# Last part of a graph network kernel: four neighbouring vertices to a partition, the last step on GpSimd, the load ring filled at once

## What is computed

```python
# out: the convolution, (B, N, H); top1[b]: the expert of graph b; x: the layer's input (after the first layer norm)
s = jax.ops.segment_sum(out.sum(axis=1), top1, num_segments=n_exp)
ss = jax.ops.segment_sum((out * out).sum(axis=1), top1, num_segments=n_exp)
mean = s / cnt                       # one column of channels per expert
var = ss / cnt - mean * mean
y = (out - mean[top1][:, None, :]) * rsqrt(var[top1][:, None, :] + BN_EPS) * bn_gamma[top1] + bn_beta[top1]
x = _layernorm(x + relu(y), axis=-1) # over the 512 channels of each vertex
```

## Time and profile before

| what | us |
|---|---|
| median of 3 runs | 2862.62 (2861.37 to 2863.1) |
| the profiled execution, its own time | 2865.02 |
| span of the profiled execution (first to last instruction) | 2863.3 |
| first transpose of the last part, from the span's start | 2554.66 |

### The profile page before, as it was taken

One profiled execution on the slowest core, in us unless ns is written; L12 is line 12 of the kernel. 1 busy time (PEld: TensorE's weight loads), 2 busy tenths in 40 slices (PEclk: granted clock), 3 DMA queues, 4 the chain that ended last, 5 costly groups with the idle time before them and its releaser, 6 DMA issues. The chain is left out here.

```text
span 2863.3 us, 70552 instructions
## 1 busy us (share of the span) xinstructions
PE 2685.5 (94%) x24130; PEld 2367.4 (83%) x24130; DVE 2114.0 (74%) x3938; ACT 1800.1 (63%) x6146; POOL 764.1 (27%) x431
## 2 busy tenths in 40 slices
PE   6999999999999999999999999999999999756765
PEld 6888888888888888888888888888888888545554
DVE  6877777777777777777777777777777777628776
ACT  3666666666666666666666666666666666528777
POOL 2133323322333232233323322333233222111110
PEclk9999999999999999999999999999999999867667
DMA  5445444444454454444444544454444444459887
GB/s 214 173 181 184 160 163 179 178 159 169 183 179 158 165 183 169 164 173 183 167 162 172 183 156 170 179 183 157 164 182 178 159 170 170 162 221 336 334 326 267
DMA packets 165114, 537.82 MB, mean 188 GB/s; under 512 B 15538, under 2 KB 48306, under 8 KB 122034
## 3 DMA queue, kind: packets, MB, share of 16 engines
q1 hardware_dynamic: 165042, 536.96, 51.2%
HBM read 427.84 MB, written 109.05 MB: 188 GB/s over the span
## 5 line engine op out<-in xcount | busy, mean ns | idle before, releaser
L532 ACT ACTIVATE prob<-prob,neg_max 128x128 f32<-128x128 f32 x2048 | 791.9, 394 | 5.3 <-DVE abs_max L654 5.3
L336 POOL TENSOR_TENSOR norm<-norm,constants 128x1 f32<-128x1 f32 x128 | 70.6, 551 | 1462.7 <-DVE norm L688 1462.7
L532 ACT ACTIVATION_READ_ACCUMULATOR prob<-prob,neg_max 128x1 f32 x2048 | 395.2, 193 | 0.0
L326 POOL TENSOR_TENSOR moments<-moments,conv 128x1024 f32 x128 | 310.7, 2427 | 293.7 <-ACT conv L577 195.0
L518 ACT ACTIVATE qk<-bank 128x512 f32<-128x512 f32 x256 | 152.7, 597 | 369.0 <-PE bank L345 369.0
L345 PE MATMUL bank<-xT_hi,wq_hi 128*128 128x256 f32 x1024 | 303.0, 296 | 19.7 <-DVE wk_lo L590 19.0
L626 DVE SCALAR_TENSOR_TENSOR prob<-bank,adj_in 128x512 f32<-128x512 f32 x512 | 316.7, 681 | 3.6 <-PE bank L345 3.6
L643 DVE TENSOR_TENSOR prob<-prob,inv_sum 128x2048 f32<-128x2048 f32 x128 | 293.4, 2292 | 4.4
L649 DVE TENSOR_REDUCE neg_max<-prob 128x16 f32<-128x2048 f32 x128 | 291.7, 2279 | 0.0
L654 DVE TENSOR_REDUCE abs_max<-prob 128x16 f32<-128x2048 f32 x128 | 291.7, 2279 | 0.0
L345 PE MATMUL bank<-xT_hi,wq_lo 128*128 128x256 f32 x1024 | 290.8, 284 | 0.0
(11 more groups left out here) (111 smaller groups left out, 6516.3 us busy)
## 6 DMA issues: line engine op xcount, KB each, us to landing
expert_hi<-expert_hi_scratch SPq DMA_DIRECT2D x128, 1024.0 KB, 5.0
expert_lo<-expert_lo_scratch SPq DMA_DIRECT2D x128, 1024.0 KB, 7.0
xT_in<-xT SPq DMA_DIRECT2D x64, 512.0 KB, 3.5
x_in<-x SPq DMA_DIRECT2D x128, 256.0 KB, 2.6
x_scratch<-x SPq DMA_DIRECT2D x128, 256.0 KB, 2.1
conv_scratch<-conv SPq DMA_DIRECT2D x128, 256.0 KB, 2.3
conv_in<-conv_scratch SPq DMA_DIRECT2D x32, 1024.0 KB, 7.2
x_in<-x_scratch SPq DMA_DIRECT2D x32, 1024.0 KB, 9.2
```

Source lines behind the costliest of these rows:

```text
L326: pool.tensor_tensor(acc, acc, conv[:, pv_mod(u, -5, 2), :, :].rearrange("p k d -> p (k d)"), ALU.add).then_inc(moments_added, 1)
L532: last = act.activation(prob[:, par2, h, :], prob[:, par2, h, :], ACT.Exp, bias=neg_max2[:, par2, h:h + 1], scale=2.0, accum_out=row_sum[: ...
```

## The change

Only the last part and the layout of the two scratch tensors change.

- The scratch tensors are laid out (graph, vertex, channel). A partition of a load now holds four neighbouring vertices of one graph (`by_token`): partition b * 32 + i holds vertices 4i to 4i + 3 of graph b of the group. That is 8 KB in one piece in DRAM for the loads, and now for the store to `out` as well.
- The columns of one transposed block are thus 32 vertices of each of the four graphs. All four blocks of a channel block c go to one PSUM bank, and scaling a graph's share takes a 128x4x32 operand (`per_graph`). ScalarE does all of the scaling, 16 activations a group, and nothing else. It reads the next group's expert numbers between its channel blocks; only at the first group of a pass of eight it reads four in a row.
- TensorE turns 16 blocks of group g, then turns back 16 blocks of group g - 1. `bnT` has two halves.
- VectorE no longer scales, and makes no shift; its residual adds and statistics are interleaved.
- GpSimd does the last step: after its power it runs four TENSOR_SCALARs of 128x512 (subtract the mean, multiply) in place, with the mean from `mean_var` and the factor from `rstd`.
- SP issues the loads of all eight slots before anything else. From then on it issues the store of group g, waits until the store of group g - 1 has landed, and loads group g + 7 into that slot.

```diff
-    x1_dram = nc.dram_tensor("x1_scratch", (P, B, D), F32, kind="Internal").ap()
+    x1_dram = nc.dram_tensor("x1_scratch", (B, N, D), F32, kind="Internal").ap()
...
-                    sp.dma_start(x1_dram[:, bass.ds(b, 1), :].rearrange("p b d -> p (b d)"),
+                    sp.dma_start(x1_dram[bass.ds(b, 1), :, :].rearrange("b n d -> n (b d)"),
...
+    ROWS = N // G
     NG = B // G
     RING = 8 if NG % 8 == 0 and NG > 8 else 4
-    STORE_LAG = RING // 2
-    JOIN_LAG, FINAL_LAG = 2, 8
-    ACT_GRAPHS = 3
-    assert NG % RING == 0 and NG > RING and G == 4
+    REFILL_LAG = 1
...
-    bnT = sb("bnT", [P, G, C, P])
+    bnT = sb("bnT", [P, 2, C, G, G, ROWS])
...
+    def by_token(t, lo, n):
+
+        return t[bass.ds(lo, n), :, :].rearrange("b (i j) d -> (b i) (j d)", j=G)
+
+    def flat(t, r):
+        return t[:, r, :, :].rearrange("p j d -> p (j d)")
+
+    def per_graph(ps, b):
+
+        return ps[:, :].rearrange("p (j b i) -> p j b i", j=G, b=G)[:, :, b, :]
...
+        def load(g, r):
+            sp.dma_start(flat(conv_in, r), by_token(conv_dram, g * G, G)).then_inc(ld_g[r], 16)
+            sp.dma_start(flat(x1_in, r), by_token(x1_dram, g * G, G)).then_inc(ld_g[r], 16)
+
+        for r in range(RING):
+            load(r, r)
+
         def group(k, r, live):
             g = k * RING + r
             if live(g):
-                if not isinstance(k, int) or k > 0:
-                    sp.wait_ge(st_g[r], k * 16)
-                sp.dma_start(conv_in[:, r, :, :], conv_dram[:, bass.ds(g * G, G), :]).then_inc(ld_g[r], 16)
-                sp.dma_start(x1_in[:, r, :, :], x1_dram[:, bass.ds(g * G, G), :]).then_inc(ld_g[r], 16)
-            if live(g - STORE_LAG):
-                b, r2 = g - STORE_LAG, (r - STORE_LAG) % RING
-                sp.wait_ge(finished, (b + 1) * G)
-                sp.dma_start(out[bass.ds(b * G, G), :, :].rearrange("b n d -> n b d"),
-                             x1_in[:, r2, :, :]).then_inc(st_g[r2], 16)
+                sp.wait_ge(finished, (g + 1) * G)
+                sp.dma_start(by_token(out, g * G, G), flat(x1_in, r)).then_inc(st_g[r], 16)
+            h, r1 = g - REFILL_LAG, (r - REFILL_LAG) % RING
+            if live(h) and live(h + RING):
+                sp.wait_ge(st_g[r1], 16 * ((k if r >= REFILL_LAG else k - 1) + 1))
+                load(h + RING, r1)
...
+        def group(k, r, live):
+            g = k * RING + r
+            if live(g):
+                pe.wait_ge(ld_g[r], (k + 1) * 32)
                 for c in range(C):
-                    last = pe.transpose(ps_turned[j][:, c * P:(c + 1) * P],
-                                        conv_in[:, r, j, c * P:(c + 1) * P], ident[:, :])
-                last.then_inc(turned, 1)
-            m, (_, j) = n - 1, place(s, 1)
-            if live(m):
-                wait_scaled(pe, k * RING + (s - 1) // G, j)
-                if live(m - G):
-                    pe.wait_ge(joined, m - G + 1)
-                for c in range(C):
-                    last = pe.transpose(ps_back[j][:, c * P:(c + 1) * P], bnT[:, j, c, :], ident[:, :])
-                last.then_inc(turned_back, 1)
+                    if live(g - 1):
+                        pe.wait_ge(scaled, (g - 1) * C + c + 1)
+                    for j in range(G):
+                        last = pe.transpose(ps_turned[c][:, j * P:(j + 1) * P],
+                                            conv_in[:, r, j, c * P:(c + 1) * P], ident[:, :])
+                    last.then_inc(turned, 1)
+            h = g - 1
+            if live(h):
+                pe.wait_ge(scaled, h * C + C)
+                for j in range(G):
+                    if live(h - 1):
+                        pe.wait_ge(joined, (h - 1) * G + j + 1)
+                    for c in range(C):
+                        last = pe.transpose(ps_back[j][:, c * P:(c + 1) * P],
+                                            bnT[:, (r - 1) % 2, c, j, :, :].rearrange("p b i -> p (b i)"),
+                                            ident[:, :])
+                    last.then_inc(turned_back, 1)
...
-            if live(g - 4):
-                pool.wait_ge(finished, (g - 4) * G + G)
-            pool.tensor_tensor(rstd[:, r % 4, :], var_eps[:, r % 2, :], minus_half[:, :].to_broadcast([P, G]),
+            pool.tensor_tensor(rstd[:, r % 2, :], var_eps[:, r % 2, :], minus_half[:, :].to_broadcast([P, G]),
                                ALU.pow).then_inc(rstd_made, 1)
+            pool.wait_ge(rstd_made, g + 1)
+            pool.sem_inc(rstd_seen)
+            for j in range(G):
+                pool.tensor_scalar(x1_in[:, r, j, :], x1_in[:, r, j, :], mean_var[:, r % 2, j, 0:1],
+                                   rstd[:, r % 2, j:j + 1], ALU.subtract, ALU.mult).then_inc(finished, 1)
...
+            es = [expert(g, b) for b in range(G)] if r == 0 else ahead[-G:]
+            if live(g - 2):
+                act.wait_ge(turned_back, (g - 1) * G)
+            for c in range(C):
+                act.wait_ge(turned, g * C + c + 1)
+                for b in range(G):
+                    column = bass.ds(es[b] * C + c, 1)
+                    last = act.activation(bnT[:, r % 2, c, :, b, :], per_graph(ps_turned[c], b), ACT.Identity,
                                           bias=shift_t[:, column], scale=scale_t[:, column])
-                last.then_inc(act_scaled, 1)
-            m, (r, j) = n - FINAL_LAG, place(s, FINAL_LAG)
-            if live(m):
-                if j == 0:
-                    act.wait_ge(shift_made, k * RING + (s - FINAL_LAG) // G + 1)
-                act.activation(x1_in[:, r, j, :], x1_in[:, r, j, :], ACT.Identity, bias=shift[:, r % 4, j:j + 1],
-                               scale=rstd[:, r % 4, j:j + 1]).then_inc(finished, 1)
+                last.then_inc(scaled, 1)
+                if r < RING - 1:
+                    ahead.append(expert(g + 1, c))
...
-                for c in range(C):
-                    column = bass.ds(e * C + c, 1)
-                    last = dve.tensor_scalar(bnT[:, j, c, :], ps_turned[j][:, c * P:(c + 1) * P],
-                                             scale_t[:, column], shift_t[:, column], ALU.mult, ALU.add)
+                if live(h - 2):
+                    dve.wait_ge(finished, (h - 1) * G)
+                join(h, r1, 0)
+                join(h, r1, 1)
+                take_stats(h, r1, 0)
+                join(h, r1, 2)
+                take_stats(h, r1, 1)
+                join(h, r1, 3)
+                take_stats(h, r1, 2)
+                take_stats(h, r1, 3)
+                dve.wait_ge(stats_taken, (h + 1) * G)
```

More of the change, by code:

```diff
@@ L760, in phase_two @@
     var_eps = sb("var_eps2", [P, 2, G])
[L761 to L762 removed]
+    rstd = sb("rstd2", [P, 2, G])
     ps_turned, ps_back = bank[4:8], bank[0:4]
@@ L775, in phase_two @@
     turned = sem("turned2")
-    act_scaled = sem("act_scaled")
-    dve_scaled = sem("dve_scaled")
+    scaled = sem("scaled")
     turned_back = sem("turned_back")
@@ L783, in phase_two @@
     rstd_made = sem("rstd_made2")
-    shift_made = sem("shift_made2")
+    rstd_seen = sem("rstd_seen")
     finished = sem("finished")
[L787 to L795, removed]
     def run_groups(eng, group, lag):
@@ L827, in group @@
             if live(g):
-                if not isinstance(k, int) or k > 0:
-                    sp.wait_ge(st_g[r], k * 16)
-                sp.dma_start(conv_in[:, r, :, :], conv_dram[:, bass.ds(g * G, G), :]).then_inc(ld_g[r], 16)
-                sp.dma_start(x1_in[:, r, :, :], x1_dram[:, bass.ds(g * G, G), :]).then_inc(ld_g[r], 16)
-            if live(g - STORE_LAG):
-                b, r2 = g - STORE_LAG, (r - STORE_LAG) % RING
-                sp.wait_ge(finished, (b + 1) * G)
-                sp.dma_start(out[bass.ds(b * G, G), :, :].rearrange("b n d -> n b d"),
-                             x1_in[:, r2, :, :]).then_inc(st_g[r2], 16)
-        run_groups(sp, group, STORE_LAG)
+                sp.wait_ge(finished, (g + 1) * G)
[4 more added lines that the diff above has]
+                load(h + RING, r1)
+        for r in range(RING):
+            group(0, r, lambda g: 0 <= g < NG)
+        with sp.Fori(1, NG // RING - 1, 1) as k:
+            for r in range(RING):
+                group(k, r, lambda g: True)
+        for r in range(RING):
+            group(NG // RING - 1, r, lambda g: 0 <= g < NG)
         for r in range(RING):
@@ L997, in _, with join, take_stats, group @@
-        run_graphs(dve, graph, JOIN_LAG + 2)
+        def join(h, r, j):
+            dve.wait_ge(turned_back, h * G + j + 1)
+            dve.scalar_tensor_tensor(out=x1_in[:, r, j, :], in0=ps_back[j][:, :], scalar=0.0,
+                                     in1=x1_in[:, r, j, :], op0=ALU.max, op1=ALU.add).then_inc(joined, 1)
+        def take_stats(h, r, j):
+            dve.wait_ge(joined, h * G + j + 1)
+            dve.bn_stats(stats[:, j, :], x1_in[:, r, j, :]).then_inc(stats_taken, 1)
+        def group(k, r, live):
```

(12 more changed lines are left out.)

73 lines of the change are left out of this document (10 added, 63 removed).

## The result

The changed kernel takes 2878.93 us (median of 4 runs, 2878.64 to 2883.06) against 2862.41 before: ratio 1.0057, 95% interval 1.0045 to 1.0069. It is **0.57% slower**. The forecast of 2809 and its range of 2785 to 2843 were wrong, and so was the side. The rival on GpSimd is what happened.

The account below looks back on a forecast made before the run. ScalarE's ring, with the queue close behind, was taken to set 9.01 us a group. The new queue end, 2807.7 (ScalarE's 2803.9), plus 2 gave span 2810, time 2811.7, median 2809 us; range 2785 to 2843.

Parts of the forecast that it names:

- The rival on GpSimd: GpSimd's four TENSOR_SCALARs of T us each become the bound, period 1.4 + 4T; chance 0.12, 0.08 beyond T = 1.93.
- the price of GpSimd's last step: One 128x512 TENSOR_SCALAR on GpSimd takes 0.9 us, bounds 0.54 and 2.27; GpSimd needs 5.0 us a group.
- the threshold of T = 1.93: From 1.93 us per GpSimd TENSOR_SCALAR, period 9.12, the kernel is slower than before.
- ScalarE: In the last part, 16 scalings of 0.342 us, waits and expert reads make 7.2 us a group.
- The 1.2 us for a slow read: ScalarE's slow expert-number read, 1.36 us more less a cover of about 0.2, costs 1.2 us a group.
- The 0.1 for the four reads in a row: Once in eight groups ScalarE reads four expert numbers, 2.4 us; mostly covered by activations, 0.1 us a group taken.
- TensorE: Blocked transposes put ScalarE's next turn 5.8 us behind at the lower clock, under 7.2, so hidden behind ScalarE.
- VectorE: Without the scaling, interleaved residual adds and statistics take 5.6 us a group, under 7.2.
- First store: SP issues the first store of the last part at 2576 us, 2579.4 before.
- The ring: Loading all eight slots first fills the DMA standstill from 2563 to 2575; the queue meets the first store without a gap.
- The queue: SP's DMA queue moves 83.9 MB after the first store at 365 GB/s, 229.9 us, ending at 2807.7.
- Shared access: GpSimd and two-SBUF-input VectorE instructions exclude each other; GpSimd's new step would be spared, VectorE's add reading one input from PSUM.

Follow-up runs that it names:

- The forms: Changed kernel with a different GpSimd instruction for each of a group's four last steps, output wrong for the layer norm; 2803.07 us, single time.
- the last experiment: Changed kernel with two of a group's last steps on GpSimd and two on ScalarE, three groups behind; 2804.4 us, ratio 0.9782.

## Why the prediction was wrong

**The step that failed** is the price of GpSimd's last step: "I take 0.9, nearer to the CAST, since one tensor is read." It takes 2.077 us. The bounds, 0.54 to 2.27, held it; the choice between them did not. The rival's formula was nearly right: period 1.4 + 4T gives 9.7 for 2.08, measured are 1.25 from the power's start to the first step's and 8.21 for the four steps, 9.46. Its sum at T = 2.08 is a span of 2576 + 31 x 9.72 + 4.7 = 2882, measured 2876.7; two errors stand against each other in it, the period 0.26 too long and a first store that stays at 2576 although the same four steps stand ahead of it (2579.3). Beyond the threshold of T = 1.93 the kernel is slower, as it said; the threshold itself no run tests. I gave that side 0.09. The kernel with the step alone (2878.5), the two of the changed kernel without it on GpSimd (2845 on ScalarE, 2801 on VectorE) and the one with three quarters of it there (2818) show the cause.

Why the choice was bad: a CAST converts and has none of the two operations, and the two TENSOR_TENSOR rows had two inputs, which I read as the reason for their price. The forms show that a scalar operand is no relief (1566 with one operation). The Trainium skill, GPSIMD Engine Reference, section 4.1 Engine selection, calls one-input work roughly line-rate there; for this TENSOR_SCALAR the traces of this case do not agree: at 537 ns on VectorE against 2077 on GpSimd the ratio is 3.9. Its advice, elementwise on VectorE, holds more strongly here than its numbers.

**Point by point.** *ScalarE*: 16 scalings without a hole take 33.91 us for 96, 5.65 a group; that is 0.353 for each, hand-overs included, where 0.342 stood, so pieces of 32 columns cost 0.2 us a group at most. The 1.2 us for a slow read was wrong: only 3 of the changed kernel's 128 reads took over 0.6 us, and the last experiment has 34 such reads that don't show in its period of 7.0. The 0.1 for the four reads in a row was too small where ScalarE is the limit. *TensorE* is not the limit in the changed kernel: right; at the lower clock no run tests its 5.8 us alone. *VectorE*: 5.69 us from group 0 to group 1 (first adds at 2563.93 and 2569.62) for 5.6. *First store*: 2579.3; less the difference of four GpSimd steps, 4 x 1.16, it would be 2574.7, against 2576. *The ring*: the standstill is gone, as said; its worth can show only in kernels in which nothing slower stands behind. *The queue*: the second wrong number. With the step on VectorE the mixed rate is 421 and 426 GB/s until 2700, not 365, and 405 in the 50 us behind, at the same share (what lowers it isn't known). The set-up's stretches were read wrongly in part: from 90 to 95 us 174 of 336 packets are under 8 KB; from 38 to 44.5 nearly all have 8 KB, and why they moved only 358 stays open. The error is against the change and so didn't show. *Shared access*: by the Trainium skill, SBUF — State Buffer, section "SBUF: two separate sides", a VectorE instruction with two SBUF inputs and a GpSimd one exclude each other for a whole instruction. The trace agrees with what the prediction made of it: VectorE's add, with one input from PSUM, kept its 0.68 beside GpSimd. But two instructions with one SBUF tensor as input did grow: the small TENSOR_SCALAR L988 from 0.17 to 0.57 us (at most 0.65), the 128x512 one from 537 to a mean of 725 ns (at most 809 in that run). None waited for a whole instruction of 2.08 us.

With the step on VectorE the chip gives 2801, near the forecast of 2809. The large gain that was forecast exists, and one instruction hides it. But that the two numbers lie close is luck: the forecast rests on a queue at 365 GB/s and a ScalarE at 7.2 us a group, and in that kernel the queue moves 421 and VectorE sets 7.07. How the changed kernel would run with T = 0.9 no run shows.

## What to carry to other kernels

Before a step moves to an engine, its very form must have a price on that engine; rows of other forms bound it, but between bounds a factor of four apart nothing chooses, and the chances should be spread over them. An idle engine is not a cheap one: 210 us of 240 idle were there, and four steps of 2.08 us a group filled them and more. When a change bundles several parts and the time doesn't move, take out the dearest instruction of the newly busy engine first: here that turned 0.6% slower into 2.2% faster.

## What was not expected of the hardware

- GpSimd's TENSOR_SCALAR of 128x512 with two operations takes 2077 ns, one operation 1566, a TENSOR_TENSOR with a broadcast second input 1041; VectorE's with two operations 537.
- ScalarE's reads of a register from SBUF, 0.28 us before SP's first store, took up to 1.70 us in 28 to 45 of 128 cases in kernels with 7 to 8.4 us a group, but only in 3 of 128 in the changed kernel. The period doesn't decide it: with GpSimd's step alone in the kernel before, at the same 9.46 us, it was 28 of 96. Nor do SP's issues just ahead alone: in the kernel before all 29 slow reads begin within 3 us of one, in the version with VectorE 13 of 37 begin later. What does stays open.
- Reads that stand in a row at the head of a loop's pass are not hidden: four of them, two of them slow, with their register instructions kept ScalarE idle for 5.07 us where it was the limiting engine.
